# A decoder layer on one core: output projection as three single-pass products, interleaved tiles of the last batch, and filler matmuls at the end

## The reference

```
q, k, v = x @ Wq, x @ Wk, x @ Wv                 # 16 heads of 128
q, k    = rmsnorm(q) * q_rms_w, rmsnorm(k) * k_rms_w
scores  = q @ k.T / sqrt(128) - distance * slope[head], causal
y       = rmsnorm(softmax(scores) @ v) * subln_w
x1      = layernorm(x + concat_heads(y) @ Wproj)            # Wproj: 2048 x 256
attn    = softmax((ctx @ XWq.T + bq) @ (ctx @ XWk.T + bk).T)
x2      = layernorm(x1 + x1 @ attn)
xq      = x2 rounded to 8 bits by its row's largest value; weights rounded to -1, 0, 1
h       = sigmoid(xq @ w_gate.T) * (xq @ w_up.T)            # 1024 wide
out     = layernorm(x2 + quantised(h) @ w_down.T)
```

## Time and profile before

| | |
|---|---|
| median of 3 runs | 432.35 us (432.35 to 432.9) |
| profiled execution | 433.11 us, its span in the trace 431.3 us |
| TensorE busy | 400.9 us, 93% |
| TensorE weight loads | 368.1 us, 85% |
| VectorE, ScalarE, GpSimd busy | 298.5, 281.4, 181.0 us |
| mean granted TensorE clock | 0.971 of full speed |

### The profile page before, as it was taken

How to read it: one execution, slowest core, us unless ns; L and a number is a source line. 1 busy time by engine, 2 the same in 40 slices (tenths; PEclk the granted TensorE clock), 3 DMA queues, 4 the chain that set the end, 5 groups by cost and what they waited for, 6 DMA issues and landing times.

```text
span 431.3 us, 8778 instructions
## 1 busy us (share of the span) xinstructions
PE 400.9 (93%) x2610; PEld 368.1 (85%) x2620; DVE 298.5 (69%) x933; ACT 281.4 (65%) x800; POOL 181.0 (42%) x283
## 2 busy tenths in 40 slices
PE   4699999999999999999999999999999999997653
PEld 3599998999999998999999998999999999986421
DVE  4678878876777577767576576667575676675695
ACT  3287876677777587667857587667757577764251
POOL 3676766633334333335435333335344343322301
PEclk9699999999999999999999999999999999999885
DMA  7999200000000000000002000000000000000000
GB/s 192 276 296 325 71 1 2 2 0 15 0 26 2 2 2 2 0 2 0 2 2 61 2 0 3 0 2 2 1 2 26 0 2 1 2 2 2 1 24 24
DMA packets 21662, 14.84 MB, mean 34 GB/s; under 512 B 1648, under 2 KB 21360, under 8 KB 21616
## 3 DMA queue, kind: packets, MB, share of 16 engines
q1 hardware_dynamic: 20800, 13.90, 11.1%
q10 hardware_dynamic: 816, 0.39, 0.3%
HBM read 13.24 MB, written 1.05 MB: 33 GB/s over the span
## 4 chain that ended last, share of the span: by engine, by line
PE 87%; DVE 7%; issue 2%; POOL 1%; DMA 1%; ACT 1%; POOLq 0%; DVEq 0%; ACTq 0%
PE ps L504 31%; PE ps L546 12%; PE ps L514 7%; PE ps L527 7%; PE ps L521 5%; PE ps L526 3%; PE ps L533 3%; PE ps L535 3%; PE ps L534 3%; PE ps L554 3%; PE ps L467 2%; PE ps L455 1%; DMA x_sb<-in_x 1%; PE ps L477 1%; PE ps L416 1%
## 5 line engine op out<-in xcount | busy, mean ns | idle before, releaser
L376 POOL TENSOR_TENSOR qk_rstd<-qk_sum,minus_half 128x2 f32<-128x2 f32 x128 | 92.8, 725 | 115.3 <-DVE qk_sum L829 114.7
L504 PE MATMUL ps<-w_hi,xT_hi 128*128 128x384 f32 x256 | 101.7, 399 | 4.1 <-DVE qk_n L823 2.3
L829 DVE TENSOR_REDUCE qk_sum<-sq 128x2 f32<-128x258 f32 x128 | 53.9, 421 | 74.2 <-ACT sq L709 70.2
L709 ACT ACTIVATE sq<-ps 128x256 f32<-128x256 f32 x128 | 49.3, 386 | 74.2 <-PE ps L504 74.1
L504 PE MATMUL ps<-w_hi,xT_lo 128*128 128x384 f32 x256 | 87.2, 342 | 0.0
L371 POOL TENSOR_TENSOR y_rstd<-y_sum,minus_half 128x2 f32<-128x2 f32 x64 | 47.3, 740 | 94.8 <-DVE y_sum L1067 93.2
L504 PE MATMUL ps<-w_lo,xT_hi 128*128 128x384 f32 x256 | 86.9, 341 | 0.0
L823 DVE TENSOR_TENSOR qk_n<-ps,qk_rstd 128x256 f32<-128x256 f32 x128 | 53.9, 421 | 33.4 <-POOL qk_rstd L376 33.2
L546 PE MATMUL ps<-wp,yT 128*128 128x256 f32 x256 | 66.0, 380 | 1.1 <-ACT yT L737 1.1
L504 PEld LDWEIGHTS ps<-w_hi,xT_hi 128*128 128x128 f32 x256 | 49.3, 193 | 8.0 <-issue 2.5
L504 PEld LDWEIGHTS ps<-w_lo,xT_hi 128*128 128x128 f32 x256 | 49.2, 193 | 1.3 <-POOL w_lo L331 0.3
(11 more groups left out here) (184 smaller groups left out, 780.1 us busy)
## 6 DMA issues: line engine op xcount, KB each, us to landing
wp<-in_L_attn_Wproj SPq DMA_DIRECT2D x4, 512.0 KB, 5.9
x_sb<-in_x SPq DMA_DIRECT2D x4, 256.0 KB, 3.4
ff_raw<-in_L_ffn_w_gate SPq DMA_DIRECT2D x1, 1024.0 KB, 7.9
ff_raw<-in_L_ffn_w_up SPq DMA_DIRECT2D x1, 1024.0 KB, 10.4
w_raw<-in_L_attn_Wq SPq DMA_DIRECT2D x4, 256.0 KB, 7.1
w_raw<-in_L_attn_Wk SPq DMA_DIRECT2D x4, 256.0 KB, 5.7
w_raw<-in_L_attn_Wv SPq DMA_DIRECT2D x4, 256.0 KB, 5.6
ff_raw<-in_L_ffn_w_down SPq DMA_DIRECT2D x1, 1024.0 KB, 8.1
```

The costliest lines, as they stand in the source:

```text
L376: pool.tensor_tensor(qk_rstd[:, t, :], qk_sum[:, t, :], minus_half[:], ALU.pow).then_inc(s_rs[t], 1)
L504: last = pe.matmul(ps[:, t, 0:W3], xa[:, b % 2, k, tok], wa[:, h, k * W3:(k + 1) * W3], start=(i == 0), stop=(i == len(parts) - 1))
L709: act.activation(sq[:, t, :, 0:D], ps[:, t, 0:2 * D].rearrange("p (a d) -> p a d", a=2), ACT.Square).then_inc(s_sq[t], 1)
L829: dve.tensor_reduce(qk_sum[:, t, :], sq[:, t], AX.X, ALU.add).then_inc(s_ss[t], 1)
```

## The change

1. **Projection.** wp and yT are split in high and low parts. ScalarE copies wp_raw to wp_hi (one head in each of the steps 3 to 18), GpSimd subtracts to get wp_lo, ScalarE writes yT_hi where it wrote yT, VectorE makes yT_lo in each step ahead of sums(n, 0). project makes three single-pass products for each tile in place of one f32 product, and waits for yT_lo.
2. **Storage.** To make room, prob is written over score, v_sb has three buffers and not four, attn one and not two, qcT and kcT lie in attn_raw, hq lies over x1 and x1T. The last batch has tiles of its own (`late`), in the storage of w_raw.
3. **Tail.** The operations of VectorE on the two tiles of the last batch are interleaved, each waiting for the one it needs (`mark`). Scales (gate_up_scale, up_127, down_scale) go from VectorE to GpSimd, the last norm of batch 2 and more of the rounding to ScalarE. TensorE turns xq of both tiles before the gates, and interleaves the turns and the down products of the hidden tiles.
4. **Fillers.** keep_busy makes products of 512 columns into a bank that is not read: 5 in each of the last two iterations, 8 before x1 is turned, 8 after the held down product, 16 after the gates, 2 between the down halves.

```
+                if t == 1 and 0 <= n - 3 < H:
+                    h = n - 3
+                    pool.wait_ge(s_wphi, h + 1)
+                    pool.tensor_tensor(wp_lo[:, h], wp_raw[:, h], wp_hi[:, h].bitcast(F32),
+                                       ALU.subtract).then_inc(s_wplo, 1)
...
             def project(n):
                 b, h = divmod(n, H)
-                pe.wait_ge(s_yT, n + 1)
+                pe.wait_ge(s_yTlo, n + 1)
                 if h == 0:
                     wait(pe, s_res1, b)
-                if b == 0 and h % 4 == 0:
-                    pe.wait_ge(s_wp[h // 4], 16)
+                if b == 0:
+                    pe.wait_ge(s_wplo, h + 1)
                 for t in range(TT):
-                    last = pe.matmul(total[:, t * C:(t + 1) * C], yT[:, n % 2, t * P:(t + 1) * P], wp[:, h, :],
-                                     start=(h == 0 and t == 0), stop=(h == H - 1), skip_group_check=True)
+                    for i, (ya, wa) in enumerate(((yT_hi, wp_hi), (yT_hi, wp_lo), (yT_lo, wp_hi))):
+                        last = pe.matmul(total[:, t * C:(t + 1) * C], ya[:, n % 2, t * P:(t + 1) * P], wa[:, h, :],
+                                         start=(h == 0 and t == 0 and i == 0), stop=(h == H - 1 and i == 2),
+                                         skip_group_check=True)
                 last.then_inc(s_pr, 1)
...
+            FILL = (8, 8, 16, 2, 5)
+            def keep_busy(bank, count):
+                for _ in range(count):
+                    pe.matmul(ps[:, bank, :], ident16[:], wgT[:, 0, 0:BANK], start=True, stop=True)
...
+                if n >= STEPS + 2:
+                    keep_busy(0, FILL[4])
                 if 0 <= n - 4:
                     project(n - 4)
...
+            keep_busy(0, FILL[0])
...
+            keep_busy(3, FILL[1])
             for t in range(TT):
                 pe.wait_ge(s_xq, tiles_done(LAST, t))
...
                 last.then_inc(s_tq, 1)
+            for t in range(TT):
                 pe.wait_ge(s_xqT, t + 1)
...
+            pe.wait_ge(s_sig, 1)
+            keep_busy(0, FILL[2])
+            turn_hidden(0, 0)
+            turn_hidden(0, 1)
+            down_half(0, 0)
+            keep_busy(3, FILL[3])
+            turn_hidden(1, 0)
+            down_half(0, 1)
+            turn_hidden(1, 1)
+            down_half(1, 0)
+            down_half(1, 1)
...
+                if n in (STEPS + 2, STEPS + 3):                 # ScalarE rounds the held hidden tiles
+                    t = n - STEPS - 2
+                    act.wait_ge(s_hs, LAST)
+                    act.activation(early.hid[:, t], early.hid[:, t], ACT.Identity, scale=h_inv[:, t:t + 1],
+                                   bias=round_col[:]).then_inc(s_hr2, 1)
...
+            round_half(0, 0)                                    # ScalarE
+            round_half(0, 1)
+            copy_half(0, 0)
+            round_half(1, 1)
+            copy_half(0, 1)
+            copy_half(1, 0)
...
+                if 0 <= n - 4 < STEPS:                          # VectorE
+                    m = n - 4
+                    dve.wait_ge(s_yT, m + 1)
+                    dve.scalar_tensor_tensor(out=yT_lo[:, m % 2], in0=ps_yT, scalar=sub_scale,
+                                             in1=yT_hi[:, m % 2].bitcast(F32), op0=ALU.mult,
+                                             op1=ALU.subtract).then_inc(s_yTlo, 1)
...
+            added0 = add_cross(0)                               # VectorE, the tail
+            dve.wait_ge(s_dve, added0)
+            stats0 = take_stats(late.res, one(0))
+            added1 = add_cross(1)
+            aggregate(1, one(0), stats0)
+            dve.wait_ge(s_dve, added1)
+            stats1 = take_stats(late.res, one(1))
+            centred0 = centre(0)
+            aggregate(1, one(1), stats1)
+            largest(0, centred0)
+            centred1 = centre(1)
+            scale_of_x2(0)
+            largest(1, centred1)
...
+            made00 = hidden_half(0, 0)
+            made01 = hidden_half(0, 1)
+            largest_half(0, 0, made00)
+            found0 = largest_half(0, 1, made01)
+            made10 = hidden_half(1, 0)
+            found0 = largest_hidden(0, found0)
+            made11 = hidden_half(1, 1)
+            scale_of_hidden(0, found0)
+            hidden_quantiser(0)
+            largest_half(1, 0, made10)
+            found1 = largest_half(1, 1, made11)
+            clip_half(0, 0, 1)
```

More of the change, by code:

```diff
@@ L97, in decoder_kernel @@
         dist = sb("dist", [P, 3 * P])
-        wp = sb("wp", [P, H, C])
-        yT = sb("yT", [P, 2, T])
+        wp_hi = sb("wp_hi", [P, H, C], F32R)
+        with nc.sbuf_tensor("wp_raw", [P, H, C], F32) as wp_raw:
+            pass
+        wp_lo = sb("wp_lo", [P, H, C], F32R)
+        yT_hi = sb("yT_hi", [P, 2, T], F32R)
+        yT_lo = sb("yT_lo", [P, 2, T], F32R)
         ident = sb("ident", [P, P])
@@ L126, in decoder_kernel @@
         ctxT = sb("ctxT", [P, T])
-        qcT = sb("qcT", [P, T])
-        kcT = sb("kcT", [P, T])
         attn_raw = sb("attn_raw", [P, TT, T])
-        attn = sb("attn", [P, 2, TT, T])
+        qcT, kcT = attn_raw[:, 0], attn_raw[:, 1]
+        attn = sb("attn", [P, TT, T])
         neg_xmax = sb("neg_xmax", [P, TT])
@@ L591, in _, with turn_hidden, down_half @@
             HALF = FC // 2
+            def turn_hidden(t, half):
+                pe.wait_ge(s_hq, 2 * LAST + 2 * t + half + 1)
+                for f in range(HALF):
+                    of = (half * HALF + f) * P
+                    last = pe.transpose(bank16(4 * t + 2 * half)[:, f * P:(f + 1) * P], late.hq[:, t, of:of + P],
+                                        ident16[:])
+                last.then_inc(s_th, 1)
+            def down_half(t, half):
+                if t == 1 and half == 1:
+                    pe.wait_ge(s_hT_dve, 1)
+                else:
+                    pe.wait_ge(s_hT, 2 * t + half + 1)
+                for f in range(half * HALF, (half + 1) * HALF):
+                    last = pe.matmul(ps[:, 4 * t + 1, 0:C], late.hT[:, t, f, :], wdT[:, f, :], start=(f == 0),
+                                     stop=(f == FC - 1))
+                if half == 1:
+                    last.then_inc(s_dn, 1)
             pe.wait_ge(s_side_out, len(JOB))
@@ L618, in _ @@
                 for k in range(KC):
[L619 removed]
+                    last = pe.transpose(bank16(4 * t)[:, k * P:(k + 1) * P], late.xq[:, t, k * P:(k + 1) * P], ident16[:])
                 last.then_inc(s_tq, 1)
+            for t in range(TT):
                 pe.wait_ge(s_xqT, t + 1)
@@ L759, in _ @@
                     side_read(n, 0)
+                if 0 <= n - 3 < H:
+                    h = n - 3
+                    if h % 4 == 0:
+                        act.wait_ge(s_wp[h // 4], 16)
+                    act.copy(wp_hi[:, h], wp_raw[:, h]).then_inc(s_wphi, 1)
                 if n in (5, 6, 7):
@@ L840, in take_stats, with aggregate @@
                 taken[0] += 1
-            def aggregate(i, sel):
-                dve.wait_ge(s_stats, taken[0])
+                return taken[0]
+            def aggregate(i, sel, count=None):
+                dve.wait_ge(s_stats, taken[0] if count is None else count)
                 for t in range(sel.start, sel.stop):
@@ L1144, in _, with centre, largest @@
+            def centre(t):
                 dve.wait_ge(s_mv[1], tiles_done(LAST, t))
-                centre_x2(t)
-            for t in range(TT):
-                quantise_centred(t)
+                return mark(dve.tensor_scalar(late.res[:, t], late.res[:, t], mean_var[:, 1, t, 0:1], None, ALU.subtract))
+            def largest(t, done):
+                dve.wait_ge(s_dve, done)
+                dve.tensor_reduce(x_most[:, one(t)], late.res[:, t], AX.X, ALU.max,
+                                  apply_absolute_value=True).then_inc(s_xc, 1)
@@ new lines, in hidden_quantiser, with clip_half @@
+            def hidden_quantiser(t):
+                dve.wait_ge(s_hsc, t + 1)
+                link(dve.reciprocal(h_norm[:, one(t)], h_scale[:, one(t)]))
+                dve.wait_ge(s_u127, t + 1)
+                dve.tensor_scalar(h_inv[:, one(t)], h_norm[:, one(t)], up_127[:, one(t)], None, ALU.mult).then_inc(s_hs, 1)
+            def clip_half(t, f, rounded):
+                dve.wait_ge(s_hr, rounded)
+                cols = slice(f * BANK, (f + 1) * BANK)
+                clip(late.hq[:, t, cols], late.hid[:, t, cols]).then_inc(s_hq, 1)
@@ new lines, in _ @@
+            clip_half(0, 1, 2)
+            scale_of_hidden(1, found1)
+            hidden_quantiser(1)
+            dve.wait_ge(s_hs, LAST + TT)
+            first = late.hid[:, 1, 0:BANK]
+            link(dve.tensor_scalar(first, first, h_inv[:, 1:2], ROUND, ALU.mult, ALU.add))
+            clip(late.hq[:, 1, 0:BANK], first).then_inc(s_hq, 1)
+            clip_half(1, 1, 3)
+            dve.wait_ge(s_th, 4)
```

(2 more changed lines are left out.)

349 lines of the change are left out of this document (187 added, 162 removed).

## The result

The changed kernel takes **427.04 us** (median of 4 runs, 426.95 to 427.24) against 432.35 for the kernel before. The ratio on record for the two is 0.9869, its 95% interval 0.9855 to 0.9883; the quotient of the two medians is 0.9877 and lies inside it. The profiled execution took 426.95 us with a span of 425.2, where it was 431.3. So the change is worth 5.3 us by the medians, 5.6 by the ratio and 6.1 by the spans. One execution of experiment 8 (508.85 us, its profiled one, at a mean granted clock of 0.76) and one of the kernel before (438.72 us, timed beside experiment 9) were disturbed and are in none of the ratios. The forecast of 422.7 had the sign; it promised 9.7 us.

A forecast was written before the change was run, and what follows sets the result against it. It took TensorE to bound the loop in about two steps of three, VectorE's chain the rest. Terms -6.1 + 0.8 - 0.5 - 1.9 - 2.0 = -9.7 us, from 432.35 to 422.7; range 419.0 to 428.8, likeliest case 420 to 425.5.

The forecast's parts named there:

- GpSimd's 16 wp_lo subtractions: Loop: they fit GpSimd's idle 0.96 us between second power and y_rstd; cost nothing, or 1.6 us in all at most.
- Piece of 0.112 us, gain 0.196 a step: Projection: six single-pass products at 0.112 us each replace 0.868 us of f32 products, gaining 0.196 us a step.
- rival A: Projection: weight loads hold single-pass pieces at 0.176 us, so six take 1.06 and the time is 438.4 us; chance 0.08.
- Loop -6.1 from step 4 on: Loop: 38 steps gain 0.18 us each, steps 5, 10, 12, 36 and 52 lose a little; -6.1 us.
- Waiting steps give nothing: Loop: in 19 steps TensorE's load waits for VectorE's qk_n, so the wait grows by 0.196 us; 17 of them give 0.
- Rival D: Loop: waiting steps gain too because VectorE's chain starts earlier; 11.8 us in the loop, time 417.0 us; chance 0.05.
- yT_lo hidden but in steps 5, 10, 12: Loop: VectorE's idle time covers yT_lo, except steps 5, 10, 12 (0.2 us worse each) and 36, 52 (0.05 each).
- rival B: Loop: VectorE becomes the bound through yT_lo, so the loop gives nothing and the time is 428.7 us; chance 0.12.
- S to the first hidden part, S + 7.0: Last batch: from the first cross addition (S), the first hidden part comes after 7.0 us, where it took 8.9; -1.9 us.
- H to the last take_down, H + 11.5: Last batch: from the first hidden part (H), the last take_down comes after 11.5 us, where it took 13.5; -2.0 us.
- Tail -3.6: After the loop: drain +0.8, clock -0.5, first hidden part -1.9, last take_down -2.0; a gain of 3.6 us.
- rival C: Tail: fillers don't hold TensorE's clock or stand in the way, so the time is 424.7 us; chance 0.13.

The follow-up runs named there:

- experiment 8: Changed kernel with one more GpSimd subtraction of 128 columns, into a tile nobody reads, before each wp_lo; 428.38 us, ratio 0.9895.
- experiment 9: Changed kernel with wp_lo moved behind y_rstd and an unread GpSimd power of two elements where the subtraction had been, in 16 steps; 423.85 us, ratio 0.9796.
- experiment 2: Changed kernel without VectorE's 64 yT_lo operations, the third product reading yT_hi; 424.31 us, ratio 0.9812.
- experiment 5: Changed kernel with the 16 wp_lo subtractions one step later, behind y_rstd or the first tile's power; 423.09 us, ratio 0.9774.
- Experiments 1: Changed kernel without GpSimd's 16 wp_lo subtractions, the second product reading wp_hi again; 422.71 us, ratio 0.9780.
- experiment 3: Changed kernel with the f32 projection of the kernel before, keeping the changed storage, tail and fillers; 428.53 us, ratio 0.9909.
- experiment 4: Changed kernel with all five filler counts at zero; 429.57 us, ratio 0.9938.
- experiment 6: Changed kernel with batch 0 on the f32 projection and wp split in steps 19 to 35, beside batch 1; 425.82 us, ratio 0.9837.

## Why the prediction was right in sign and missed by 4.3 us

**The step that failed** is "GpSimd's 16 wp_lo subtractions (w_lo's form, 0.73) fall between the second power and y_rstd, where GpSimd idles 0.96. That leaves 0.2, so I take nothing, and 0.1 a step, 1.6 us in all, as the other end". The idle time was read on GpSimd alone. What counted was what VectorE did in it: casts and rounding steps from SBUF to SBUF (the core's memory), which take about twice as long beside the subtraction.

By the means in 30 to 120, VectorE lost 9 x 0.22 + 8 x 0.36 + 0.36 = 5.2 us more than before; 3.9 us reached TensorE in steps 4 to 19 (+3.08 against -0.80 with the work moved), and by experiment 2 some 1.2 us of this, an estimate, need yT_lo beside it. The whole term measures 4.1 us by the ratios of experiment 5, where I had 0 and at most 1.6. Experiments 1 (out: 3.8 back), 5 (moved: 4.1 back) and 9 (a power in its place: at most 0.86 lost) tell this from the late power, and so do steps 13 to 18: they hold 1.6 of the 3.9 us, and the power behind wp_lo isn't late in them.

How the two engines share their access to SBUF I can't see in these rows; that a VectorE operation waits, I can. The Trainium skill (SBUF — State Buffer, "SBUF: two separate sides" and "Who interferes with whom") says that the two engines share a pair of ports, that VectorE's casts and tensor_scalar operations can use it too, and that whichever starts first holds it for its whole instruction. By that the cast of step 12 should end at 77.92 + 0.55 = 78.47; it ended at 78.33. The trace agrees to 0.14 us. Experiment 9 does not agree: the power of 0.69 us started 0.03 ahead of the cast, by the rule the cast would have ended 0.69 + 0.55 = 1.24 us after the power's start, and it ended 0.61 after. So, as far as GpSimd's rough rows tell, the length of its row isn't the length for which it holds VectorE; here the measurement decides.

A sign of it could be read before the run. The kernel before, VectorE and GpSimd from 80.25, the one place in 30 to 120 where this rounding step met a w_lo:

```profile
80.25 0.81 POOL L326 TENSOR_TENSOR w_lo<-w_raw,w_hi 128x256 fp32r<-128x256 f32 x1
80.50 0.84 DVE L1025 TENSOR_SCALAR ff_raw<-ff_raw 128x512 f32<-128x512 f32 x1
```

0.84 where its neighbours take 0.43: one row of the same line with another duration, and the price of a meeting could be read from it, 0.4 us. Sixteen meetings would have given 6.6 us as the other end where I had 1.6.

**Point by point.**
- *Piece of 0.112 us, gain 0.196 a step:* 0.118 measured, so six take 0.71 and a step gains 0.16, which is what the free steps gave. Nearly right; rival A (0.176) is out.
- *Loop -6.1 from step 4 on:* -1.67 (3.08 - 4.75); with wp_lo moved -5.57. There the 38 free steps gave 0.16 each instead of 0.18 (0.85 us less in all), and steps 5, 10 and 12 cost 0.85 together instead of 0.6. On the other side the waiting steps gave 0.4 instead of nothing, and 36 and 52 gave 0.05 instead of costing 0.1. These make the 0.5 between -6.1 and -5.57.
- *Waiting steps give nothing:* right for most. In experiment 5 twelve of the seventeen others than 10 and 12 keep their length within 0.03 us; 14, 19, 21 and 22 are 0.08 to 0.15 shorter and 32 is 0.08 longer. Rival D wanted 0.196 from each and is out.
- *yT_lo hidden but in steps 5, 10, 12:* right in experiments 1 and 5 (+0.21 to +0.38 each). In the changed kernel it wasn't, in batch 0 only, because the widened operations had used up the holes. Hence the result lies near rival B's number, 428.7, without being B: from step 20 on the loop gave 4.75. That 427.04 is inside 419.0 to 428.8 is luck in part: the room that I had left for B holds it, and not a term that I had right.
- *The band of the likeliest case, 420 to 425.5:* it doesn't follow from its own terms. 1.6 us and a piece of 0.121 (0.054 us less gain in each of 38 steps, 2.1) lead to 426.4, a tail better by one to 421.7. The measured time is above both upper ends. Halfway from the forecast to D is 419.9, not 419.0.
- *Smaller storage edits at nothing:* right (experiment 3, within 0.02 us a step).
- *Drain +0.8:* from the load of step 63 to take_projection it was 11.09 and is 11.95: +0.86.
- *Clock, -0.5:* take_projection to the first cross addition 5.55 before, 5.13 after: -0.42.
- *S to the first hidden part, S + 7.0:* 409.68 - 402.67 = 7.01, -1.93.
- *H to the last take_down, H + 11.5:* 420.46 - 409.68 = 10.78, so -2.75 and not -2.0. The two h_inv came at H + 4.3 and H + 6.9, where I had 4.65 and 7.5.
- *Tail -3.6:* -4.2, so an error of 0.6 in its favour hides a part of the loop's. Last take_down at 17.8 us behind the first cross addition. The line under "what would show it" said 16.5, which does not agree with my own 7.0 + 11.5; the working was right and that number wrong.
- *Fillers hold the clock:* right, 1.00 in every window from 400 to 420 (0.79 from 420 to 425, where TensorE has only 0.12 us left to do); rival C is out. But what they are worth was too small: I had 2.0 us for it in all, and experiment 4 measures 3.0 of the tail's 3.9. The sum gave 3.9 to the interleaving and 0.5 to the clock, so its split was wrong where its total was nearly right.

**Still open.** Up to step 3, ahead of anything the change does, the profiled kernels differ from the kernel before by -0.7 to +0.3 us. One profile each can't say why. And which part of a GpSimd instruction holds VectorE, and by how much for each kind and width, no run here tells.

## What to carry to other kernels

Idle time on GpSimd is free only if VectorE is doing nothing there that GpSimd can hold. Before putting a wide GpSimd operation in a hole, read VectorE's rows over the same stretch; here a reduction and operations that read PSUM kept their times, while a cast and a rounding step from SBUF to SBUF took about twice as long. The same sixteen instructions cost 4.1 us in one hole and nothing measurable in the next, one step later. And when a total comes short, look at the mean durations of instructions that nobody edited: that view pointed to the cause before any experiment.

## What the runs showed of the hardware

- A subtraction of 256 columns on GpSimd (0.74 us) beside a cast of 768 columns on VectorE: the cast goes from 0.55 to 1.13 us; a rounding step of 512 columns from 0.43 to 0.84; an operation on two elements from 0.17 to 0.53. A power of two elements on GpSimd that lasts nearly as long (0.69) leaves the cast at 0.58.
- It works the other way too: wp_lo took 1.14 us and not 0.74 beside a VectorE operation of 1024 columns (experiment 6). GpSimd's w_lo, 0.73 elsewhere, took 1.22 at 76.00 in the changed kernel, right behind the start (75.93) of a VectorE product of two SBUF tiles with 512 columns.
- Single-pass products of 256 columns, each with its own weight load of 0.19 us, go every 0.118 us at a granted clock of 1.00.
- With 44 products that nobody reads the granted clock was 1.00 in every window from 400 to 420; without them it was 0.55, 1.00, 0.66 and 0.81 in these four, and the time 3.0 us more. Without the last ten of the loop alone it was 0.66 from 395 to 400 and again 1.00 from 400 to 420.
